# Leaving out four runs of bf16 products on the identity in the front of an eight-group decoder kernel

## The reference

```python
x = ln(x + L0_attn(x))    # causal attention with one head, weights qkv and o_proj
x = ln(x + L0_xattn(x))   # long convolution of products of x and context, 16 filters k, skip term
x = ln(x + L0_ffn(x))     # ternary weights w1, w2, w3, activations quantised to 8 bits
x = ln(x + L1_attn(x))    # gated recurrence: cumulative sum with decay, group norm, Wo
x = ln(x + L1_xattn(x))   # cross attention, 16 query heads, 4 key/value heads of 128, RMS norm on q and k
x = ln(x + L1_ffn(x))     # gated FFN with e4m3 products and bf16 results
```

## Time and profile before

| what | value |
|---|---|
| time, median of 3 (lowest to highest) | 866.34 us (865.15 to 866.76) |
| profiled execution: time, span | 863.91 us, 861.4 us |
| TensorE matmul busy | 813.6 us (94%), 5004 instructions |
| TensorE weight load busy | 632.2 us (73%) |
| VectorE busy | 650.6 us (76%) |
| ScalarE busy | 529.4 us (61%) |
| GpSimd busy | 328.4 us (38%) |
| mean granted TensorE clock | 0.989 of full |
| bf16 products on the identity (line 1096) | 194, of them 138 in the first 75 us |

### The profile page before, as it was taken

How to read it: one execution, slowest core, us unless ns; L and a number is a source line. 1 busy time by engine, 2 the same in 40 slices (tenths; PEclk the granted TensorE clock), 3 DMA queues, 4 the chain that set the end, 5 groups by cost and what they waited for, 6 DMA issues and landing times.

```text
span 861.4 us, 14691 instructions
## 1 busy us (share of the span) xinstructions
PE 813.6 (94%) x5004; PEld 632.2 (73%) x5004; DVE 650.6 (76%) x1696; ACT 529.4 (61%) x1315; POOL 328.4 (38%) x419
## 2 busy tenths in 40 slices
PE   6599999899999999999999999999999999999984
PEld 5466576588878777787778778887788778867762
DVE  2367768797888887888688888888888877745654
ACT  4464723555674687628774687438763687668763
POOL 1267676672346214452253233431562332202110
PEclk9699999999999999999999999999999999999998
DMA  8956223001001100110011000110010001000000
GB/s 287 365 179 205 75 74 122 13 2 26 1 14 49 26 1 13 62 26 2 13 62 26 1 13 12 51 26 1 14 50 1 1 1 50 13 1 2 13 1 24
DMA packets 40520, 41.25 MB, mean 48 GB/s; under 512 B 19072, under 2 KB 34944, under 8 KB 40064
## 3 DMA queue, kind: packets, MB, share of 16 engines
q1 hardware_dynamic: 40448, 40.33, 14.3%
HBM read 31.93 MB, written 8.39 MB: 47 GB/s over the span
## 4 chain that ended last, share of the span: by engine, by line
PE 75%; ACT 10%; DVE 8%; SPq 2%; POOL 2%; issue 2%; DMA 1%; POOLq 0%; DVEq 0%; ACTq 0%
PE bank L1338 11%; PE bank L1377 10%; PE bank L1356 6%; PE bank L1090 6%; PE bank L1298 6%; PE bank L1366 5%; PE bank L1161 3%; PE bank L1159 3%; PE bank L1162 3%; PE bank L1361 2%; PE bank L1231 2%; PE bank L1191 2%; PE bank L1344 2%; PE bank L1244 2%; ACT S L719 2%
## 5 line engine op out<-in xcount | busy, mean ns | idle before, releaser
L1338 PE MATMUL bank<-XTE,w_xq 128*128 128x256 f32 x512 | 122.2, 382 | 2.4 <-ACT QA L711 1.2
L719 ACT ACTIVATE S<-S,mx 128x128 f32<-128x128 f32 x256 | 99.4, 395 | 32.0 <-DVE mx L1021 31.5
L1377 PE MATMUL bank<-w_xo,OX 128*128 128x256 f32 x512 | 116.0, 380 | 0.0
L1338 PEld LDWEIGHTS bank<-XTE,w_xq 128*128 128x128 f32 x512 | 93.9, 190 | 19.4 <-ACT QA L711 3.6
L1377 PEld LDWEIGHTS bank<-w_xo,OX 128*128 128x128 f32 x512 | 95.8, 190 | 13.0 <-issue 0.5
L710 ACT ACTIVATE QS<-bank,per_partition_sb 128x256 f32<-128x256 f32 x128 | 60.7, 475 | 63.5 <-PE bank L1338 63.4
L1018 DVE SCALAR_TENSOR_TENSOR S<-bank,rq,xmask 128x128 f32<-128x128 f32 x256 | 71.6, 342 | 18.8 <-PE bank L1356 17.8
L310 POOL TENSOR_TENSOR prod<-XTA,ccolA 128x256 f32<-128x256 f32 x96 | 58.9, 645 | 31.7 <-PE bank L1162 21.4
L1356 PEld LDWEIGHTS bank<-KTX,QA 128*128 128x128 f32 x512 | 62.5, 191 | 11.2 <-issue 9.1
L1356 PE MATMUL bank<-KTX,QA 128*128 128x128 f32 x512 | 68.4, 279 | 0.2
L1366 PE MATMUL bank<-PT,VX 128*128 128x512 f32 x128 | 66.1, 609 | 0.1
(11 more groups left out here) (233 smaller groups left out, 1857.7 us busy)
## 6 DMA issues: line engine op xcount, KB each, us to landing
keys_spilled<-KTX SPq DMA_DIRECT2D x6, 512.0 KB, 2.7
values_spilled<-VX SPq DMA_DIRECT2D x6, 512.0 KB, 3.6
KTX<-keys_spilled SPq DMA_DIRECT2D x6, 512.0 KB, 3.6
VX<-values_spilled SPq DMA_DIRECT2D x6, 512.0 KB, 4.5
xin<-in_x SPq DMA_DIRECT2D x8, 256.0 KB, 2.7
taps_sb<-in_taps SPq DMA_DIRECT2D x1, 2048.0 KB, 11.7
cnat<-in_ctx SPq DMA_DIRECT2D x8, 256.0 KB, 2.8
ccolA<-in_ctxT SPq DMA_DIRECT2D x32, 64.0 KB, 2.7
```

The costliest lines, as they stand in the source:

```text
L719: ins = nc.scalar.activation(S[:, b, seq(h)], S[:, b, seq(h)], ACT.Exp, bias=mx[:, b, h:h + 1], accum_out=sm[:, b, h:h + 1])
L1338: ins = nc.tensor.matmul(cols(EQ)[:, h], w_xq[:, k, hh * XDIM:(hh + 1) * XDIM], XTE[:, k], start=k == 0, stop=k == HALVES - 1)
L1377: ins = nc.tensor.matmul(rows(EY)[:, b], OX[:, h, b], w_xo[:, n * XGROUP + h], start=n == 0 and h == 0 and b == 0, stop=n == XKV - 1 and h ...
```

## The change

The four calls of `keep_clock` in `front` are left out, with the wait on `pool_const` that stood ahead of the first. The call in `output` stays, and so do the order strings, since none of the calls was a piece of its own.

```diff
@@ -1116,9 +1116,6 @@
                 sig(ins, "a_sc")
-                if g == 0:
-                    pe.wait_ge(sems["pool_const"], 2)
-                    keep_clock(EY, 24)
                 yield
@@ -1130,8 +1127,6 @@
                 sig(ins, "a_y")
-                if g == 0:
-                    keep_clock(EY, 30)
                 yield
@@ -1167,8 +1160,6 @@
                 sig(ins, "b_oT")
-                if g == 0:
-                    keep_clock(EY, 60)
```

## The result

The changed kernel took 868.39 us (median of 15 executions, 866.83 to 869.1), the kernel before 865.21 us beside it (15, 863.59 to 867.41). The ratio is 1.0029, 95% interval 1.002 to 1.0038: slower by 2.5 us (1.7 to 3.3); the two medians lie 3.2 us apart, within that interval. The forecast was 870.7 us, 4.4 us up. The direction and the range held, the size was well over what was measured.

A forecast was written before the change was run, and what follows sets the result against it. PE, almost never idle behind the front, was taken to bound the kernel, so its delay there counts whole. Front 0.7, DVE's hold 1.6 and clock fall 2.1 gave +4.4 us on the median 866.34: 870.7 us, range 866.1 to 872.6.

The forecast's parts named there:

- First call, nothing: At 18.32 us, 24 products fill idle time in a 7.65 us gap; removing them changes nothing.
- Third call, 1.34 us on PE's path, weights there: Behind the skip product, 40.19 us: removing 24 products gains 1.34 us, since the key weights landed by 38.1 us.
- Second call, 1.95 us for the clock: Behind the product with V, 33.45 us: without it full clock returns at 43.2 us, not 37.0; loss 1.95 us.
- front term s: Shift of everything up to the convolution's end from second and third call together: +0.7 us, between -0.6 and +1.4.
- row of 3.0 to 5.4 us for the clock's return: Time at half speed after PE's work starts again, read from the profile: 3.0 to 5.4 us.
- Fourth call, gain of 0.40 at POOL's root: Behind the convolution PE gains 3.35 us, but POOL is busy until 80.02 us, so the main chain gains only 0.40.
- Bias under line 893, 2.2 us: POOL's bias of the next keys now falls over DVE's scalings and holds them by the shared port: 2.2 us lost.
- A pause of 4.9 us, the clock falls, 2.1 us: PE idles about 4.9 us ahead of line 1216's transposes, then restarts at half speed: 2.1 us lost, from 1.5 to 2.7.
- the forecast's own signs: Right: PE idle nearly 5 us before line 1216, second clock fall near 85 to 88 us. Wrong: pause under 3 us.
- rival B: DVE is held at line 893 but the clock stays up through PE's 4.9 us pause: 868.6 us; chance 0.15.
- A: The forecast itself: DVE is held and PE's pause drops the clock: 870.7 us, range 868.3 to 872.6; chance 0.55.
- Carried whole: Behind the front PE is busy 67.1 of 68.5 us, so a delay at 91.5 us delays the end equally.

The follow-up runs named there:

- the filler: Changed kernel with 36 bf16 products on the identity put into PE's last pause ahead of line 1207: 866.41 us, ratio 1.0 [0.9986, 1.0015].
- the filler near the end: Changed kernel with 24 bf16 products put into PE's 1.57 us pause near 831 us, last group but one: 868.43 us, ratio 1.0024 [1.0009, 1.0039].
- the reordered queue: Changed kernel with SyncE's first spill of keys and values issued ahead of the last staged weight's load: 868.83 us, ratio 1.0029 [1.0015, 1.0042].
- the trace without the front calls: Kernel before with first, second and third call left out, the fourth kept: 865.32 us, ratio 0.999 [0.9977, 1.0003].

## Why the prediction was right in direction and wrong in size

- **First call, nothing.** Right: the next product waits for ACT in every trace.
- **Third call, 1.34 us on PE's path, weights there.** Right in the mechanism. 0.9 us measured, with 1.3 in its interval.
- **Second call, 1.95 us for the clock.** This is the step that failed. "What it bought is the clock at 37.0 us" is true of the traced execution, and in such a one the term is right (+2.18 us in the trace without it). Over the executions it is worth 0.2 us (-1.0 to 1.4); in some the clock falls again behind the call, as two of the traces show. The front term s was +0.7 and measured -0.9 (-2.0 to +0.3). That 1.6 us is most of what parts 4.4 from 2.5. The forecast read the loss against one execution that kept its clock and put it onto a median over executions that need not have, as the trace without the fourth call shows for the same front. Its row of 3.0 to 5.4 us for the clock's return was short as well: in the eight traces it took 3.9 to 6.9 us from line 1084's start.
- **Fourth call, gain of 0.40 at POOL's root.** Right: root of c at 80.61 us against 80.45 before with s = 0.62, so 0.46 gained.
- **Bias under line 893, 2.2 us.** Right in place and nearly in size: 3.23 - 1.14 = 2.09. The place was partly luck: the slack of 1.5 us that was counted on was gone, for PE's keys came 1.5 us later than the forecast's 3.35 us gain would have them. PE's resumption was forecast at 86.4 + 0.6 = 87.0 and came at 86.76; the shift without s was 1.3 and not 1.6.
- **A pause of 4.9 us, the clock falls, 2.1 us.** The sum of the pause was right (1.42 + 0.38 + 2.96 = 4.76), but ACT's wait for the spill's DMA and its copies, left out in the working, broke it in three. By the forecast's own signs (a pause under 3 us is wrong, a fall near 85 to 88 us is right) the changed kernel's trace speaks against this term: its last pause is 2.96 us and the clock held. The fall came in other executions: 1.7 us in each of the two traces that have it, 2.4 us by the filler. The changed kernel's own trace looks like rival B, the executions together like A.
- **The tail.** Not foreseen: a fall at 832 us that costs 1.35 us in the trace. Traces of kernels that were ahead of before have it too, so it is not the change's doing as far as the traces go; how often the kernel before has it is not known. The filler there won 0.4 us, not told from nothing.
- **Carried whole.** Right: 1.93 us at 112 us, 1.95 at 808.

With the measured sizes the sum is -0.9 + 1.3 + 2.0 = 2.4 us, beside the ratio's 2.5. The 2.0 is what is left of the fourth call's 3.3 us when the trace's 1.3 is taken off, about 1 us to either side; it lies between the 1.7 of one fall and the filler's 2.4, and is not known better than that. The forecast was further put on a median of three executions (866.34), 1.1 us above the median of 15. Put on the traced execution, the same sum gives 868.3, next to the measured 868.39; that agreement is luck, as the front's term shows.

## What to carry to other kernels

A filler run that looks hidden may be holding an engine back, and so keeping a later transfer or a neighbour's instruction out of the way: before removing it, ask which engine's queue runs free, and beside which of its neighbour's instructions its own then fall. A gain or loss by the clock that one trace shows is one draw; read half-clock time over many executions before it becomes a term of a sum. Here the first three calls together are worth nothing that could be told, and the kernel without any call and with one wait on POOL is 0.9 to 1.9 us faster than the one with all four.

## What the runs showed of the hardware that was not expected

The times at which the clock falls and returns stand elsewhere in each execution against the kernel's start. The first fall came at 23.4, 24.1, 25.3 and 26.7 us in the four traces with the first call, and from 20.2 to 23.4 us in the nine without it. Nearly the same pauses (1.1 to 1.4, 0.38 and 3.0 to 3.3 us) kept the clock in two traces (the changed kernel, twice) and lost it in two (the reordered queue, the filler near the end). And a run of 30 products ended with the clock back at 35.5 us, only for it to be lost at 38.9. The clock can also fall within steady work: in the trace without the front calls it was at half from 164.1 to 167.5 us, behind pauses of PE of 0.5 to 0.8 us, and the shift of line 788 went from -0.6 to +0.7 us over it. The clock column reads 1.00 before its first record, while 12 f32 transposes at 6.92 us in the changed kernel take 2.82 us, where eight take 1.15 us at full clock (76.89 us).
